# Side work of a causal attention block, moved to other units and in front of single maxima

## The chip, the core and the metric

The program runs on one core of a Trainium2 chip. A core has five engines, each with its own instruction queue: TensorE (PE in the profile, its weight loads apart as PEld), VectorE (DVE), ScalarE (ACT), GpSimd (POOL) and SyncE (SP), which here only issues transfers. An engine takes its instructions in the order of its queue, and waits on semaphores that other engines or transfers raise. The metric is the device time of one execution in microseconds (us); smaller is better.

## The reference

For x of 4 batches x 1024 rows x 128 columns, three residual blocks are computed in float32. The mixture-of-experts block stands before and after the attention.

```
x = x + 0.5 * ffn(layernorm(x))       # router top 2 of 8, 1280 places per expert, 128 -> 512 -> 128, exact gelu
x = x + attn(layernorm(x))            # 16 heads of 8, causal softmax, output projection
x = x + 0.5 * ffn(layernorm(x))       # same weights

# attn
q, k, v = split(x @ wq.T + bq), split(x @ wk.T + bk), split(x @ wv.T + bv)
scores  = einsum('bhsd,bhtd->bhst', q, k) / 8 ** 0.5, causal mask
ctx     = einsum(softmax(scores), v);  out = ctx @ wo.T + bo

# the router of ffn, for all 4096 rows n
logits = xt @ gate_w;  top_logits, top_idx = top_k(logits, 2);  weights = softmax of the two
rank of a row in its expert = number of rows before it that chose it (all first choices, then all second)
a choice counts if rank < 1280; out[n] = sum of its weights * expert output
```

## The kernel before, in words

The first ffn comes first, then the attention over the 4 batches, then the second ffn. The change touches the attention alone. It has 16 steps: batches 0 to 3, and in each the groups g = 0 to 3 of four heads. Batches 1 and 2 are the same code ("mid"), batch 0 is "first" and batch 3 "final".

A step has 12 units u. Units 0 to 3 are the first half of the queries with key blocks 0 to 3 (queries of width 512, 384, 256, 128), units 4 to 11 the second half with key blocks 0 to 7 (512 for units 4 to 8, then 384, 256, 128). In each unit PE makes two pairs of score blocks (L1489), ACT takes their exponentials (L1823), for the units on the diagonal (0 to 3 and 8 to 11) POOL puts the causal zeros in (L2252), and two units later PE multiplies them with the values (L1537, called "values" below). Beside this, the row maxima of the *next* step are computed: PE makes score blocks (L1505, diagonal mask L1514), and DVE reduces them (L1903, "a maximum" below). Units 0 to 11 hold 2, 2, 1, 1, 2, 2, 2, 2, 2, 2, 2 and 0 of the 20 maxima. POOL splits the maxima of a half into three bf16 parts (`split_max`, L2226 to L2230: half 1 of this step's successor at u = 11, half 0 at u = 7), PE turns them (L1548, at the ends of units 0 and 8), and SP moves them through memory into the query tiles.

Scores and maxima share a ring of three two-bank slots in PSUM, in the order score, maximum, score, maximum, so PE can write a block only when ACT or DVE has read the block three places earlier. One more bank (`c_bank`) serves all small tasks in a fixed order. At the end of unit 11 and of unit 2 DVE normalises the context (`context`, L1913 and L1915), which frees that bank for L1548.

The side work of the neighbouring batches is placed by conditions on (g, u) in each engine's `step`, as a rule *behind* the unit's exponentials or maxima:

- g = 0: POOL adds the expert outputs to x1 of the next batch; DVE takes its row statistics (`sums`, `moments`), POOL the root (`rstd1`), ACT normalises it (`norm`, L1797, 8 row tiles at u = 10 and 11). For the batch before, PE and DVE add the output projection (`add_out`), and DVE takes router statistics (`router_sums`, u = 8 to 11, then `router_moments`).
- g = 1: POOL takes the router's root, ACT normalises the router's rows (`norm_out`, L1808, u = 1 and 2); x, q and k tasks of the next batch at u = 3 to 10.
- g = 2: the router: logits on PE at u = 5, on DVE the first choice behind u = 6, the second behind u = 7, ranks behind u = 9, places behind u = 10, weights and row numbers behind u = 11.
- g = 3: 16 scatters of the router's rows on POOL (`router_scatter`, L404), 3 behind each of u = 0 to 3 and 1 behind each of u = 4 to 7; v tasks at u = 3 and 4.

A dependent chain of DVE operations runs through `Steps`: each call raises a semaphore and waits for it. It is written so, and the scatters are placed so:

```
def __call__(self, ins):
    ins.then_inc(self.s, 1)
    self.k += 1
    self.eng.wait_ge(self.s, self.base + self.k)
...
turns = range(3 * u, 3 * u + 3) if u < 4 else range(u + 8, min(u + 9, TOPK * T))
```

## Time and profile before

| | |
|---|---|
| three runs | 1027.87, 1031.98, 1039.04 us; median 1031.98 us |
| the profiled execution | 1036.6 us from its first to its last instruction (no other time is given for it) |
| attention, first exponential of batch 0 to that of the last step | 290.2 to 789.7 us |
| busy, whole span | PE 831.8 us (80%), DVE 601.5 (58%), ACT 523.4 (50%), POOL 489.6 (47%) |
| DVE L1903, the maxima | 320 instructions, 348.5 us |
| ACT L1823, the exponentials | 384 instructions, 300.4 us |
| POOL L404, the scatters | 48 instructions, 47.4 us |

The span is read by step: a step begins where ACT starts the exponentials of its unit 0. "[0.97 <-DVE ctx L1915]" behind a row means that the engine sat idle for 0.97 us before it, until that instruction was done. PEclk is the granted clock of TensorE, 1.00 for 2.4 GHz and 0.50 for 1.2 GHz.

### The profile page before, as it was taken

How to read it: one execution, taken by the hardware profiler on the slowest of the kernel's cores; microseconds unless marked ns; L12 is line 12 of the kernel's file. 1: busy time of each engine (PE TensorE's matmuls, PEld its weight loads, DVE VectorE, ACT ScalarE, POOL GpSimd, SP SyncE). 2: the span in 40 equal slices, each digit the busy share in tenths (PEclk: the TensorE clock that was granted, in tenths of full speed). 3: DMA queues.
4: the chain of work that ended last, by engine and by line, in shares of the span. 5: the costliest groups of instructions: out<-in, count | busy, mean ns of one | idle time of the engine just before them, and what ended most of it. 6: DMA issues, size and time to landing. Idle time of an engine off the chain costs nothing. (4 is left out here: it accounts for less than half of the span.)

```text
span 1036.6 us, 18080 instructions
## 1 busy us (share of the span) xinstructions
PE 831.8 (80%) x6599; PEld 446.5 (43%) x6599; DVE 601.5 (58%) x1237; ACT 523.4 (50%) x841; POOL 489.6 (47%) x686
## 2 busy tenths in 40 slices
PE   8569999944668988888978899878887618999990
PEld 7437878742212223332333323323232316787770
DVE  7931211124767788888787977878775423334235
ACT  6323343442237776777556786566766303433330
POOL 5047455325652662646467522562224651545453
PEclk9769999986657999999799999999899758999995
DMA  7115575621451262341524224323202124423236
GB/s 204 73 26 153 148 217 145 192 63 51 130 162 66 53 189 48 89 144 43 174 76 105 99 53 152 85 65 106 53 18 79 53 63 149 130 79 97 78 136 228
DMA packets 96185, 110.81 MB, mean 107 GB/s; under 512 B 12279, under 2 KB 68763, under 8 KB 96104
## 3 DMA queue, kind: packets, MB, share of 16 engines
q1 hardware_dynamic: 84752, 88.86, 29.1%
q0 software_dynamic: 9216, 17.98, 6.8%
q10 hardware_dynamic: 2136, 2.91, 0.8%
q8 instruction: 49, 0.80, 0.3%
q14 instruction: 32, 0.26, 0.1%
HBM read 57.86 MB, written 52.89 MB: 107 GB/s over the span
## 5 line engine op out<-in xcount | busy, mean ns | idle before, releaser
L1903 DVE TENSOR_REDUCE m_blk<-banks 128x8 f32<-128x1024 f32 (+1 forms) x320 | 348.5, 1114 | 79.7 <-PE banks L1505 67.1
L1823 ACT ACTIVATE pt<-banks 128x1024 f32<-128x1024 f32 (+3 forms) x384 | 300.4, 811 | 145.1 <-PE banks L1489 142.7
L1537 PE MATMUL banks<-pt,vs 128*32 128x512 f32 (+3 forms) x1536 | 176.6, 534 | 7.2 <-POOL pt L2252 3.8
L1489 PE MATMUL banks<-qb,kp 64*128 64x512 bf16 (+3 forms) x768 | 132.6, 351 | 53.7 <-DVE m_blk L1903 45.2
L2252 POOL TENSOR_SCALAR_AFFINE_SELECT pt<-pt 128x512 f32<-128x512 f32 x128 | 81.6, 637 | 192.1 <-ACT pt L1823 191.7
L1505 PE MATMUL banks<-kp,qa 64*128 64x128 bf16 (+4 forms) x1152 | 126.4, 294 | 19.6 <-ACT pt L1823 11.6
L849 POOL DMA_INDIRECT xe<-xn_rows,slot_tok x80 | 79.9, 999 | 94.4 <-PE banks L1190 37.2
L675 POOL DMA_INDIRECT y_tab<-ys,ids x70 | 68.0, 972 | 81.5 <-DVE ys L635 64.5
L1106 ACT ACTIVATE he<-banks,b_up 128x512 f32<-128x512 f32 (+1 forms) x96 | 57.9, 616 | 89.9 <-PE banks L1190 89.5
L1505 PEld LDWEIGHTS banks<-kp,qa 48*128 48x128 bf16 (+1 forms) x1152 | 46.2, 99 | 130.3 <-ACT pt L1823 92.7
L585 ACT ACTIVATE hT<-banks,bfc 128x512 f32<-128x512 f32 (+1 forms) x96 | 56.3, 615 | 84.9 <-DVE bfc L607 48.8
L1489 PEld LDWEIGHTS banks<-qb,kp 64*128 64x128 bf16 x768 | 36.1, 95 | 134.5 <-DVE m_blk L1903 89.5
L1190 PE MATMUL banks<-xeT,w_up 128*128 128x512 f32 (+1 forms) x192 | 76.3, 548 | 2.3 <-DVE xeT L1018 2.3
L1200 PEld LDWEIGHTS banks<-w_dn,he 128*128 128x128 f32 x640 | 73.9, 192 | 3.8 <-issue 3.8
L1200 PE MATMUL banks<-w_dn,he 128*128 128x128 f32 x640 | 75.2, 275 | 0.0
L632 DVE TENSOR_TENSOR ys<-banks,early_b 128x512 f32<-128x512 f32 (+1 forms) x24 | 14.5, 603 | 88.7 <-PE banks L543 88.7
L1027 DVE TENSOR_TENSOR ye<-banks,b_dn 128x512 f32<-128x512 f32 (+1 forms) x24 | 14.5, 603 | 83.2 <-PE banks L1200 83.2
L1537 PEld LDWEIGHTS banks<-pt,vs 128*32 128x32 f32 x1536 | 31.3, 111 | 54.1 <-issue 31.9
L404 POOL DMA_INDIRECT bucket<-rows,row_ix x48 | 47.4, 988 | 13.8 <-issue 13.8
L1190 PEld LDWEIGHTS banks<-xeT,w_up 128*128 128x128 f32 x192 | 37.2, 202 | 29.7 <-issue 24.2
L2265 POOL DMA_INDIRECT gy<-y_slots,y_row x32 | 32.6, 1018 | 36.0 <-POOLq L711 26.7
L1018 DVE COPY xeT<-banks 128x512 f32<-128x512 f32 (+1 forms) x24 | 14.3, 597 | 46.7 <-PE banks L1181 46.7
(344 smaller groups left out, 1128.8 us busy)
## 6 DMA issues: line engine op xcount, KB each, us to landing
bucket<-zero SPq DMA_DIRECT2D x16, 660.0 KB
qb<-q_stack SPq DMA_DIRECT2D x32, 192.0 KB, 3.5
qa<-q_stack SPq DMA_DIRECT2D x30, 192.0 KB, 3.3
kp<-k_stack SPq DMA_DIRECT2D x30, 192.0 KB, 4.2
q_stack<-qp SPq DMA_DIRECT2D x18, 256.0 KB
k_stack<-kq SPq DMA_DIRECT2D x18, 256.0 KB
y_slots<-ye SPq DMA_DIRECT2D x16, 256.0 KB, 2.5
mid<-x SPq DMA_DIRECT2D x8, 512.0 KB, 3.6
```

The source lines that it names most:

```text
L585: nc.scalar.activation(hT[par][:, b, 0:n * P], h_bank[b][:, 0:n * P], ACT.Gelu, bias=bfc[q][:, b:b + 1]).then_inc(h_done, 1)
L675: nc.gpsimd.indirect_dma_start(table[:, :], bass.IndirectOffsetOnAxis(ap=ids[q][:, t:t + 1], axis=0), ys[q][:, t, :], None, bounds_check=r ...
L849: nc.gpsimd.indirect_dma_start(xe[q][:, t, :], None, xn_rows[:, :], bass.IndirectOffsetOnAxis(ap=slot_tok[:, e * CT + t:e * CT + t + 1], a ...
L1106: nc.scalar.activation(he[par][:, b, 0:n * P], h_bank[b][:, 0:n * P], ACT.Gelu, bias=b_up[q][:, b:b + 1]).then_inc(up_done, 1)
L1190: nc.tensor.matmul(h_bank[b][:, 0:n * P], w_up[q][:, b * P:(b + 1) * P], xeT[q][:, t0 * P:(t0 + n) * P], start=True, stop=True).then_inc(u ...
L1200: i = nc.tensor.matmul(y_bank[par][:, t * P:(t + 1) * P], he[par][:, b, t * P:(t + 1) * P], w_dn[q][:, b, :], start=b == 0, stop=b == FB - 1)
L1489: i = nc.tensor.matmul(ring[SLOT["score", 2 * u + pair]][:, s, 0:w], kp[g][rows_s, pair, kb * P:(kb + 1) * P], qb[par][rows_s, pair, q0:q0 ...
L1505: i = nc.tensor.matmul(ring[slot][:, s, at:at + blocks * P], qa[par][rows_s, pair, qt * P:(qt + 1) * P], kp[g][rows_s, pair, kb * P:(kb + ...
L1537: i = nc.tensor.matmul(o_bank[VW * h:VW * h + VW, q:q + w], vs[par][:, kb, h, :], pt[u % PTS][:, h, 0:w], start=u in (0, SECOND), stop=u i ...
L1823: nc.scalar.activation(pt[u % PTS][:, 2 * pair:2 * pair + 2, 0:w], ring[SLOT["score", 2 * u + pair]][:, :, 0:w], ACT.Exp, scale=SCALE).the ...
L1903: nc.vector.tensor_reduce(dst, ring[slot][:, :, 0:blocks * P].rearrange("p s (j k) -> p s j k", k=P), AX.X, ALU.max).then_inc(m_done, 1)
L2252: nc.gpsimd.affine_select(out=v, in_=v, compare_op=ALU.is_ge, fill=0.0, base=0, pattern=[[0, HS], [1, P]], channel_multiplier=-1).then_inc ...
```

## The change

`router_top2`, `router_second`, `router_rank`, `router_places` and `router_weights` become two generators, `router_choose` and `router_rank`. `Steps.later` puts the `yield` between an instruction and the wait for it, so that what the caller places there stands ahead of the wait. Four tables say which row tiles are handled in which (g, u). The number of instructions stays the same.

```diff
+            def later(self, ins):
+                ins.then_inc(self.s, 1)
+                self.k += 1
+                yield
+                self.eng.wait_ge(self.s, self.base + self.k)
...
+            NORM_AT = {(0, 10): (0, 3), (0, 11): (3, 5), (1, 2): (5, T)}
+            OUT_AT = {(1, 10): (0, 3), (1, 11): (3, 5), (2, 2): (5, T)}
+            SUMS_AT = {(6, 0): (0, 2), (6, 1): (2, HB), (7, 0): (HB, 6), (7, 1): (6, T)}
+            ROUTER_SUMS_AT = {(0, 9): (0, 2), (0, 10): (2, 4), (0, 11): (4, 6), (1, 3): (6, T)}
...
-                        if g == 0 and not bt.final and u >= 10:
-                            norm(b + 1, (u - 10) * T // 2, (u - 9) * T // 2)
-                        if g == 1 and not bt.first and 1 <= u <= 2:
-                            norm_out(b - 1, (u - 1) * T // 2, u * T // 2)
+                        if (g, u) in NORM_AT and not bt.final:
+                            norm(b + 1, *NORM_AT[g, u])
+                        if (g, u) in OUT_AT and not bt.first:
+                            norm_out(b - 1, *OUT_AT[g, u])
...
+                        if g == 2 and not bt.first and u == 6:
+                            out_task(at, "r_lg", b - 1)
+                        if g == 2 and not bt.first and u == 10:
+                            out_task(at, "r_rk", b - 1)
                         for m in range(M_FROM[u], M_FROM[u + 1]) if more else ():
+                            if not bt.first and ((g == 2 and 6 <= u <= 10) or (g == 3 and u == 2)):
+                                for _ in range(2):
+                                    next(held["run"], None)
+                            if g == 0 and not bt.final and (u, m - M_FROM[u]) in SUMS_AT:
+                                sums(b + 1, *SUMS_AT[u, m - M_FROM[u]])
+                            if g == 0 and not bt.final and u == 8:
+                                (moments, moments_end)[m - M_FROM[u]](b + 1)
                             reduce(n + 1, m, SLOT["max", m])
...
-                        if g == 0 and not bt.first and u == NU - 1:
+                        if g == 1 and not bt.first and u == 4:
                             router_moments(dve, (b - 1) * ROUTER_STEPS)
-                        if g == 1 and not bt.first and u == 0:
+                        if g == 1 and not bt.first and u == 8:
                             router_numbers(dve, 0, b - 1).then_inc(r_num, 1)
...
+                        if g == 2 and not bt.first and u in (9, 11):
+                            for _ in range(4 if u == 9 else 2):
+                                next(held["run"], None)
+                        if g == 3 and not bt.first and u == 2:
+                            for _ in held["run"]:
+                                pass
...
-                        if g == 1 and not bt.first and u == 0:
+                        if g == 1 and not bt.first and u == 5:
                             router_rstd(pool, b - 1)
                             router_shift(pool, b - 1)
-                        if g == 3 and not bt.first:
-                            if u == 0:
+                        if g == 3 and not bt.first and u > 2:
+                            if u == 3:
                                 wait_apart(pool, r_idx, b)
...
-                                turns = range(3 * u, 3 * u + 3) if u < 4 else range(u + 8, min(u + 9, TOPK * T))
+                                turns = range(3 * u - 9, min(3 * u - 6, TOPK * T))
```

On POOL, g = 3 of batches 1 and 2, from the mask of unit 0 of the step (before):

```order
L2252 AFFINE_SELECT pt<-pt 128x4x128 x2
L404 DMA bucket<-rows,row_ix 40960x132 x3
L2252 AFFINE_SELECT pt<-pt 128x4x128
L404 DMA bucket<-rows,row_ix 40960x132 x3
L2252 AFFINE_SELECT pt<-pt 128x4x128
L404 DMA bucket<-rows,row_ix 40960x132 x3
L2252 AFFINE_SELECT pt<-pt 128x4x128
L404 DMA bucket<-rows,row_ix 40960x132 x6
L2226 TENSOR_SCALAR m_neg<-m_of 128x16
...
L404 DMA bucket<-rows,row_ix 40960x132
L2245 COPY vs<-v_all 128x32x9
```

and with the change (L400 is the scatter, L2260 the mask, L2234 the first step of `split_max`, L2253 the copy of the values for the next step):

```order
L2260 AFFINE_SELECT pt<-pt 128x4x128 x5
L400 DMA bucket<-rows,row_ix 40960x132 x12
L2234 TENSOR_SCALAR m_neg<-m_of 128x16
...
L400 DMA bucket<-rows,row_ix 40960x132 x3
L2253 COPY vs<-v_all 128x32x9
L2260 AFFINE_SELECT pt<-pt 128x4x128
L400 DMA bucket<-rows,row_ix 40960x132
L2260 AFFINE_SELECT pt<-pt 128x4x128 x2
```

The first mask of the five is that of unit 11 of the step before. No scatter stands between the masks of units 0 to 3 any more; 12 stand ahead of `split_max` and 15 ahead of the mask of unit 8.

On DVE, the end of g = 0 and the start of g = 1 in batch 1 (before):

```order
L1908 TENSOR_REDUCE m_of<-m_blk 128x16
L277 BN_STATS stat<-x 128x6 x4
L285 BN_AGGR mv<-stat 128x2 x8
L288 TENSOR_SCALAR neg_mean<-mv 128x8
L289 TENSOR_SCALAR var_e<-mv 128x8
L1913 RECIPROCAL recip<-banks 128x16
L1915 TENSOR_TENSOR ctx<-banks,recip 128x4x32
L1903 TENSOR_REDUCE m_blk<-banks 128x2x3 x2
```

and with the change:

```order
L1910 TENSOR_REDUCE m_of<-m_blk 128x16
L284 BN_STATS stat<-x 128x6 x4
L1915 RECIPROCAL recip<-banks 128x16
L1917 TENSOR_TENSOR ctx<-banks,recip 128x4x32
...
L284 BN_STATS stat<-x 128x6 x2
L1905 TENSOR_REDUCE m_blk<-banks 128x2x4 x2
L292 BN_AGGR mv<-stat 128x2 x8
L295 TENSOR_SCALAR neg_mean<-mv 128x8
L296 TENSOR_SCALAR var_e<-mv 128x8
L1905 TENSOR_REDUCE m_blk<-banks 128x2x4 x2
```

The aggregation and the two operations behind it went from ahead of the context to unit 4 of g = 1, two of the statistics to unit 3.

On DVE, g = 2 of batch 1 from unit 6, with the change (before, the seven operations from L333 stood together, then two maxima, then the next seven):

```order
L333 TENSOR_SCALAR tok_id<-tok_id 128x8
L334 COPY lg<-banks 128x64
L340 TENSOR_REDUCE top<-lg 128x8
L1905 TENSOR_REDUCE m_blk<-banks 128x2x4
L341 TENSOR_TENSOR eq<-lg,top 128x64
L342 TENSOR_TENSOR cand<-eq,place 128x64
L1905 TENSOR_REDUCE m_blk<-banks 128x2x4
L343 TENSOR_REDUCE chosen<-cand 128x8
L344 TENSOR_TENSOR hot<-place,chosen 128x8x8
L1905 TENSOR_REDUCE m_blk<-banks 128x2x4
```

Two operations of the router now stand in front of each single maximum.

## Rows read from the trace of the kernel before

**Rows 1.** The page's first line: the profiled execution.

```profile
span 1036.6 us, 18080 instructions
```

**Rows 2.** Windows of whole steps (stretch, length, busy by engine, PEclk, DMA share, GB/s).

```profile
365.00:393.90 28.90, 24.14 (x262) 7.84 (x258) 23.28 (x27) 20.18 (x29) 15.62 (x27) 1.00 0.59 173
393.90:424.30 30.40, 25.79 (x278) 9.68 (x274) 24.40 (x29) 19.90 (x28) 7.60 (x19) 1.00 0.24 59
424.30:455.60 31.30, 27.99 (x294) 10.57 (x290) 28.15 (x56) 23.92 (x39) 20.87 (x32) 1.00 0.44 128
490.30:525.90 35.60, 32.85 (x302) 11.68 (x298) 27.21 (x47) 21.01 (x32) 15.74 (x28) 0.81 0.48 139
525.90:559.20 33.30, 25.39 (x278) 9.63 (x274) 25.31 (x35) 20.36 (x29) 23.40 (x35) 1.00 0.32 86
626.20:660.00 33.80, 28.93 (x302) 11.02 (x298) 26.95 (x47) 21.08 (x31) 7.54 (x19) 0.95 0.45 130
```

**Rows 3.** Timeline of ACT: start us, us, instruction [idle before]; starts of units 0 and 3.

```profile
626.17 1.94 ACT L1823 ACTIVATE pt<-banks 128x1024 f32<-128x1024 f32 x2 [1.09 <-PE banks L1489]
632.79 0.38 ACT L1823 ACTIVATE pt<-banks 128x256 f32<-128x256 f32 x1 [1.21 <-PE banks L1489]
...
455.56 1.91 ACT L1823 ACTIVATE pt<-banks 128x1024 f32<-128x1024 f32 x2
464.57 0.77 ACT L1823 ACTIVATE pt<-banks 128x256 f32<-128x256 f32 x2
...
590.43 1.92 ACT L1823 ACTIVATE pt<-banks 128x1024 f32<-128x1024 f32 x2
595.57 1.65 ACT L1808 ACTIVATE rows<-x,shift,rstd 128x128 f32<-128x128 f32 x4
600.06 0.38 ACT L1823 ACTIVATE pt<-banks 128x256 f32<-128x256 f32 x1 [0.34 <-PE banks L1489]
...
723.27 1.94 ACT L1823 ACTIVATE pt<-banks 128x1024 f32<-128x1024 f32 x2 [1.09 <-PE banks L1489]
733.59 0.38 ACT L1823 ACTIVATE pt<-banks 128x256 f32<-128x256 f32 x1 [0.34 <-PE banks L1489]
```

**Rows 4.** Timeline of DVE and PE at the start of g = 1, batch 3.

```profile
722.88 0.86 DVE L277 BATCH_NORM_STATS2 stat<-x 128x6 f32<-128x128 f32 x4
725.03 0.25 DVE L1913 RECIPROCAL recip<-banks 128x16 f32<-128x16 f32 x1
...
725.65 0.24 PE L1548 MATMUL banks<-identb,m_parts 128*48 128x128 bf16 x1 [0.97 <-DVE ctx L1915]
```

**Rows 5.** Timeline of DVE, g = 1 of batch 1, behind unit 5.

```profile
472.67 0.75 DVE L1989 SCALAR_TENSOR_TENSOR rest<-banks,bq_c,qp 128x512 f32<-128x512 f32 x1 [0.55 <-ACT qp L1772]
```

**Rows 6.** Timeline of PE in g = 2, batch 2.

```profile
648.76 0.39 PE L1489 MATMUL banks<-qb,kp 64*128 64x512 bf16 x2 [1.04 <-DVE m_blk L1903]
```

**Rows 7.** Timelines of POOL and PE in g = 3 of batch 1 (step from 525.9).

```profile
528.74 1.09 POOL L404 DMA_INDIRECT bucket<-rows,row_ix  x1 [0.20 <-issue]
550.55 0.22 POOL L2230 TENSOR_TENSOR m_parts<-m_neg,m_parts 128x16 bf16<-128x16 f32 x1
...
552.75 0.65 POOL L2252 TENSOR_SCALAR_AFFINE_SELECT pt<-pt 128x512 f32<-128x512 f32 x1
...
541.83 0.43 PE L1537 MATMUL banks<-pt,vs 128*32 128x128 f32 x8 [1.56 <-POOL pt L2252]
551.55 0.24 PE L1548 MATMUL banks<-identb,m_parts 128*48 128x128 bf16 x1
555.56 1.07 PE L1537 MATMUL banks<-pt,vs 128*32 128x512 f32 x8
```

**Rows 8.** The same places on PE in g = 3 of batch 0 (step from 393.9).

```profile
416.69 0.24 PE L1548 MATMUL banks<-identb,m_parts 128*48 128x128 bf16 x1
420.69 1.06 PE L1537 MATMUL banks<-pt,vs 128*32 128x512 f32 x8
```

**Rows 9.** Forms of instruction, 424 to 830 us (busy us, mean ns | idle before).

```profile
L404 POOL DMA_INDIRECT bucket<-rows,row_ix x48 | 47.4, 988 | 13.8 <-issue 13.8
```

More of the change, by code:

```diff
@@ L387, in router_places @@
+            nc.vector.tensor_tensor(tk, tk, rb[:, T * W:T * W + W], ALU.add).then_inc(evac, 1)
+            yield
+            yield from step.later(nc.vector.tensor_tensor(ranks[:], ranks[:], hot[:], ALU.mult))
+            yield from step.later(nc.vector.tensor_reduce(rank[:], ranks[:], AX.X, ALU.add))
             nc.vector.tensor_scalar(over[:], rank[:], float(CAP), SKIP, ALU.is_ge, ALU.mult)
-            step(nc.vector.tensor_tensor(place_in[:], rank[:], sign[:], ALU.mult))
-            step(nc.vector.scalar_tensor_tensor(place_in[:], chosen[:], -4.0 * CAP, place_in[:], ALU.mult, ALU.add))
@@ L390, in router_places @@
-            step(nc.vector.tensor_tensor(place_in[:], place_in[:], over[:], ALU.add))
-        def router_weights(dve, call, buf, step):
+            yield from step.later(nc.vector.tensor_tensor(place_in[:], rank[:], sign[:], ALU.mult))
+            yield from step.later(nc.vector.scalar_tensor_tensor(place_in[:], chosen[:], -4.0 * CAP, place_in[:], ALU.mult,
+                                                                 ALU.add))
+            yield from step.later(nc.vector.tensor_tensor(place_in[:], place_in[:], over[:], ALU.add))
@@ L393, in router_weights @@
             dve.wait_ge(r_exp, call + 1)
-            step(nc.vector.tensor_scalar(es[:], eg[:], 1.0, None, ALU.add))
-            step(nc.vector.reciprocal(gap[:], es[:]))
+            yield from step.later(nc.vector.tensor_scalar(es[:], eg[:], 1.0, None, ALU.add))
+            yield from step.later(nc.vector.reciprocal(gap[:], es[:]))
             nc.vector.tensor_copy(rows[buf][:, :, C_P0], gap[:])
@@ L2314, in step @@
                             mask(n, u)
+                        if g == 0 and not bt.final and u == 9:
+                            rstd1(b + 1)
                         if is_last(b, g) and u == 10:
```

94 lines of the change are left out of this document (36 added, 58 removed).

## The prediction, made before the changed kernel ran

> **What bounds the kernel now.** The profiled execution spans 1036.6 us [rows 1], above the median of the runs (1031.98), so I work out a difference on this trace and take it off the median. I read the windows by step first, then the timelines of ACT, DVE, PE and POOL where a step is longer than a plain one.
>
> A plain step, with hardly any side work, is g = 2 of batch 0: 28.9 us, of which PE is busy 24.1, DVE 23.3 and ACT 20.2 [rows 2]. No engine is full there. What bounds it is the ring of three slots: PE writes a block, ACT or DVE reads it, PE may write again. So side work costs nothing while it fits into an engine's idle time inside a unit, and costs its excess when it stands as a block in front of something that the ring waits for. The reader should see in rows 2 how far the other steps are from 28.9, or from 30.4 for g = 3 with its v tasks (batch 0, no router): 31.3 for g = 0 of batch 1, 35.6 and 33.8 for the router steps g = 2 of batches 1 and 2, 33.3 for g = 3 of batch 1. The first units of g = 1 stand out in ACT's timeline: from the start of unit 0 to that of unit 3 a step without normalisations takes 632.79 - 626.17 = 6.6 us; batches 1, 2 and 3 take 9.0, 9.6 and 10.3 [rows 3]. That is 9.1 us in all over plain.
>
> **A. Start of g = 1 (gain).** Two blocks make those 9.1 us. On DVE four statistics (0.86 us) and the aggregation chain behind them (725.03 - 722.88 - 0.86 = 1.3 us) stand ahead of the context; PE waited 0.97 us for the context in order to turn the maxima [rows 4]. On ACT two blocks of four `norm_out`, 1.65 us each or 0.41 an instruction, stand between exponentials [rows 3]. The change leaves the four statistics there and takes the 1.3 us and both ACT blocks away. What comes instead is three `norm` (3 x 0.41 = 1.2 us) behind unit 2, where ACT in the plain step is idle 1.21 us before unit 3 [rows 3]: hidden, and if it is not, PE's transposes at unit 3 are late by the excess. The 0.86 us of statistics against the 0.97 us that PE waits, less the 1.3 removed, makes PE's wait vanish, but the first maximum is still late; I take 0.45 us a batch as left. Gain 9.1 - 3 x 0.45 = 7.7 us. Bounds: none is saved beyond the 9.1; at worst the old cost stays where ACT work remains, about half, 4.5. Batch 0 loses half of its eight `norm` from the end of g = 0 as well; between nothing and the 3 x 0.41 moved away I take 0.7. A together: 8.4.
>
> **B. What g = 1 gets back (cost).** Two statistics (0.43) at unit 3 and the chain (1.3) at unit 4. In batches 1 and 2 DVE is idle 0.55 us behind unit 5, waiting for ACT's q part [rows 5], and the ring is held by ACT there, so I take 0.3 each. In batch 3 no q, k tasks run, and the step is as plain as a step is; there 1.7 us meet idle time of (28.9 - 23.3) / 12 = 0.5 us a unit [rows 2], so 1.0. `norm_out` behind units 10 and 11 (3 and 2 instructions, 1.2 and 0.8 us): plain idle time of ACT is (28.9 - 20.2) / 12 = 0.7 a unit, and unit 10 holds another cast in batches 1 and 2. Bounds 0 to 1.2 each; 0.4, as most of it is covered: 0.8. The last three stand behind unit 2 of g = 2, in the same 1.21 us as in A: 0. POOL's root and product at unit 5 stand ahead of nothing that is due before. B: 2.4 us of cost.
>
> **C. g = 0 (gain).** Batches 1 and 2: the step is 2.4 us over plain [rows 2], for PE's transposes, `add_out`, statistics and moments. The change only cuts the blocks of four statistics into twos in front of single maxima and the moments in two. Between 0 and 2.4, nearer to a third as the sum of DVE work is the same: 0.7 each, 1.4.
>
> **D. The router, g = 2 (gain).** The same DVE operations, in pairs of about 0.5 us instead of two blocks of about 1.6. In batch 2 PE waited 1.04 us for a maximum behind such a block [rows 6]. But a pair in front of a maximum in each of seven to eight places also makes DVE's period longer than its 0.5 us of idle time a unit covers, so most of the block's price comes back as many small ones. Between -1.0 and +1.0 us a step, I take a gain of 0.4 for each of three steps: 1.2. The logits on PE and what they do to the clock (0.81 and 0.95 in the two windows of rows 2) stay. On the waits inside the chain the Trainium skill speaks ("VectorE: DVE Perf Modes", "The DRAIN you can't avoid"): a semaphore between two DVE operations adds no time of its own. By it D would be 0.9, as a third of my gain is the hidden wait; the sum would move by 0.3.
>
> **E. g = 3 of batches 1 and 2 (cost).** This is the part that I trust most. Before, POOL starts the scatters 2.8 us into the step, and the masks of units 2 and 3 stand behind them: PE waited 1.56 us for one [rows 7]. The step takes 33.3 instead of 30.4 [rows 2]. Now POOL does the four masks first, and then 12 scatters, `split_max`, 3 scatters, the copy and the mask of unit 8. When is it done? Scatters take (47.4 + 13.8) / 48 = 1.28 us each in a row [rows 9]. In a plain step the exponentials of unit 3 start 6.6 us in, the second ends about 0.9 later (two of 0.38 and a gap, an estimate), the mask takes 0.65: the first scatter is at 8.5. From the first scatter to the end of `split_max` it was 550.77 - 528.74 = 22.0 us with 15 scatters and three masks; less 3 x 1.28 and 3 x 0.7 it is 16.3 (gaps between them leave 16.6). So the parts of the maxima are ready at 25.1. PE wants them at 416.69 - 393.9 = 22.8 in a step that nothing holds up [rows 8]; before, it came for them at 25.6 [rows 7]. **PE stalls 2.3 us at unit 8.** Then three scatters, copy and mask: before, 2.6 us with one scatter, so 5.2, and the mask of unit 8 ends at 30.3. PE's values for unit 8 want it at 420.69 - 393.9 = 26.8, plus the 2.3, that is 29.1; **1.2 us more**. The step comes to 30.4 + 3.5 + 0.2 for the weights' operations in front of unit 2 = 34.1, against 33.3: 0.8 worse, although the old stall is gone. The earlier context at its start (nine operations on DVE ahead of it become two) is already in the 30.4. To this I add 0.8 for the clock, which fell in some places where PE stood (rivals). E: 2 x 1.6 = 3.2 us of cost; bounds -2.9 (no stall at all) and +6 a step. Batch 3's last step has no maxima; its eight scatters keep their place: 0.
>
> **The sum.** -8.4 + 2.4 - 1.4 - 1.2 + 3.2 = -5.4 us. On the profiled execution 1031.2; on the median **1026.6 us**. The rest of the program is untouched, and the attention's end moves the second ffn's start as it is.
>
> **The rivals.**
>
> R1, *POOL's queue becomes the bound and the clock falls with it* (slower). Each stall of PE in g = 3 leaves it idle; if TensorE is granted 1.2 GHz afterwards, its values go at half speed through units 9 to 11 and into the next step. Price from rows: the router step at clock 0.81 is 1.8 us longer than that at 0.95 [rows 2]; two stalls, each with such a fall, make E's step 0.8 + 2 x 1.8 = 4.4, and a later start of the scatters (row numbers late, or a mask late) adds a us for each us. At 6 a step and with A only half as large the sum is -4.5 + 2.4 - 1.4 - 1.2 + 12 = +7.3: 1039. It decides from 1.6 + 2.7 = 4.3 us a step on. For it: the two router steps lost clock although PE is busier there than in a plain step [rows 2]. Against: in rows 7 PE waited 1.56 us and the window reads 1.00. The Trainium skill ("TensorE: Matmul & The Clock Gate", "HAM oscillation") says that a kernel whose TensorE keeps pausing for another unit falls back to 1.2 GHz again and again. By that rule R1's price comes due each time; the trace agrees only for some pauses. Chance 0.14.
>
> R2, *E costs nothing and the clock gains* (faster still). If DVE or ACT hold PE back so that it comes to unit 8 at 25 anyway, the stall is hidden, and E is -1.0 a step for the missing waits; with A's starts also go the falls of the clock, and D is worth 1.0 a step. -8.4 + 2.4 - 1.4 - 3.0 - 2.0 = -12.4: 1019.6. Against it: a plain g = 3 reaches unit 8 at 22.8. Chance 0.22.
>
> R3, *the work only changes places*. DVE's total is the same, and every unit of g = 1 and g = 2 has little idle time left; then A's gain is given back in units 3 to 11: -1 to -2 in all, 1030.5. For it: DVE is busy 27 to 28 us in each such step. Against: the waits at the start of g = 1 are for blocks that are gone. Chance 0.16.
>
> The forecast itself has 0.48.
>
> **The numbers.** The range reaches from R2's neighbourhood up into R1's: 1017 to 1037; the forecast's own runs from 1022 to 1031. Within 1% of 1031.98 is 1021.7 to 1042.3, about what a measurement tells from no change. Below it lie R2 and the lower tail of the forecast: 0.27. Above lies the tail of R1: 0.07. Between: 0.66.
>
> **What the profile would show.** A: units 0 to 2 of g = 1 take 7 us instead of 9 to 10 in batches 1 to 3, and no wait of L1548 for the context is left there. B: waits for maxima at units 4 and 5 of g = 1, in batch 3 above all. D: waits for maxima below 1 us through units 6 to 8 of g = 2, the step 33 to 35 as before. E: in g = 3 of batches 1 and 2 no wait of values for a mask at units 4 and 5, but one of 2 to 2.5 us at L1548 behind unit 8 for POOL's parts and one of about a us of values for the mask of unit 8; the step 34 to 36 us. I am wrong if g = 3 is below 32, if the starts of g = 1 stay above 8.5, or if the span outside the attention moves.

## The result

The changed kernel took 1020.0 us in the median of four runs (1017.33 to 1024.78), the kernel before beside it 1031.09 (1027.87 to 1039.04). The ratio is 0.9866, 95% interval 0.9823 to 0.9909: faster by 1.3%. The forecast was 1026.6 us. Two later comparisons of the same two kernels gave 0.9882 (0.9839 to 0.9925) and 0.9877 (0.9831 to 0.9923). A ratio with its interval is worked out from the single executions and need not be the quotient of two medians. Medians are over executions in the chip's faster state; of one version below (half of D) two of twelve executions, at 1035.77 and 1039.03 us, were in the slower one and are left out.

The profiled execution spans 1020.6 us, 16.0 less than [rows 1]. Not all of that is the change. Attention begins (first exponential of batch 0) at 284.1 us instead of 290.2, and the code up to there is the same; from there to the last step's start it is 489.0 us instead of 499.5; the rest is 247.5 against 246.9. Leave out g = 0 of batch 0 as well, whose length varies with no edit near it (below), and it is 447.2 against 458.1: **10.9 us** in the steps that the prediction speaks of.

### The profile page after: what moved, and what is told of

Read it like the earlier page. It is cut to its first block and busy times, and to the rows that moved or that the text cites. A ratio compares the mean times of both kernels' runs of the same rounds, so it can differ in the third digit from the quotient of the medians.

```text
span 1020.6 us, 18073 instructions
## 1 busy us (share of the span) xinstructions
PE 822.9 (81%) x6599; PEld 442.1 (43%) x6599; DVE 598.4 (59%) x1237; ACT 522.6 (51%) x841; POOL 489.6 (48%) x686
## 5 line engine op out<-in xcount | busy, mean ns | idle before, releaser
L1533 PE MATMUL banks<-pt,vs 128*32 128x512 f32 (+3 forms) x1536 | 174.5, 528 | 2.5 <-ACT o_sb L1765 2.4
L2260 POOL TENSOR_SCALAR_AFFINE_SELECT pt<-pt 128x512 f32<-128x512 f32 x128 | 81.4, 637 | 178.7 <-ACT pt L1825 178.6
L845 POOL DMA_INDIRECT xe<-xn_rows,slot_tok x80 | 79.9, 999 | 88.1 <-PE banks L1186 34.3
L1186 PE MATMUL banks<-xeT,w_up 128*128 128x512 f32 (+1 forms) x192 | 73.7, 533 | 2.3 <-DVE xeT L1014 2.3
L400 POOL DMA_INDIRECT bucket<-rows,row_ix x48 | 48.0, 1000 | 15.0 <-issue 14.1
L1533 PEld LDWEIGHTS banks<-pt,vs 128*32 128x32 f32 x1536 | 31.0, 110 | 48.4 <-issue 32.3
L2273 POOL DMA_INDIRECT gy<-y_slots,y_row x32 | 32.4, 1014 | 35.9 <-POOLq L707 26.7
```

Of the source, the lines that this page charges most:

```text
L845: nc.gpsimd.indirect_dma_start(xe[q][:, t, :], None, xn_rows[:, :], bass.IndirectOffsetOnAxis(ap=slot_tok[:, e * CT + t:e * CT + t + 1], a ...
L1186: nc.tensor.matmul(h_bank[b][:, 0:n * P], w_up[q][:, b * P:(b + 1) * P], xeT[q][:, t0 * P:(t0 + n) * P], start=True, stop=True).then_inc(u ...
L1533: i = nc.tensor.matmul(o_bank[VW * h:VW * h + VW, q:q + w], vs[par][:, kb, h, :], pt[u % PTS][:, h, 0:w], start=u in (0, SECOND), stop=u i ...
L2260: nc.gpsimd.affine_select(out=v, in_=v, compare_op=ALU.is_ge, fill=0.0, base=0, pattern=[[0, HS], [1, P]], channel_multiplier=-1).then_inc ...
```

## The profile after

First the page's first line and PE's row in it, then windows of whole steps (stretch, length, busy time by engine PE, PEld, DVE, ACT, POOL, granted clock, DMA share, GB/s). They are g = 0 to 3 of batch 1, g = 2 of batch 2, g = 1 and g = 2 of batch 3, and answer to [rows 1, 2].

```profile
span 1020.6 us, 18073 instructions
...
PE 822.9 (81%) x6599; PEld 442.1 (43%) x6599; DVE 598.4 (59%) x1237; ACT 522.6 (51%) x841; POOL 489.6 (48%) x686
```

```profile
417.70:448.60 30.90, 27.10 (x286) 10.44 (x282) 26.96 (x50) 22.83 (x36) 20.31 (x29) 1.00 0.42 125
448.60:482.60 34.00, 30.57 (x278) 10.06 (x274) 28.24 (x48) 27.76 (x46) 22.58 (x36) 0.95 0.30 68
482.60:516.70 34.10, 31.29 (x302) 11.65 (x298) 26.69 (x47) 22.27 (x34) 15.59 (x27) 0.85 0.49 145
516.70:551.20 34.50, 28.50 (x278) 10.18 (x274) 25.36 (x36) 19.85 (x28) 23.52 (x36) 0.90 0.35 98
614.90:647.00 32.10, 28.69 (x302) 11.02 (x298) 26.51 (x48) 22.26 (x35) 7.32 (x18) 0.95 0.47 138
711.10:742.40 31.30, 25.13 (x262) 7.90 (x258) 24.82 (x44) 22.26 (x33) 9.45 (x22) 0.95 0.23 57
742.40:773.10 30.70, 27.27 (x300) 10.88 (x296) 26.41 (x47) 22.17 (x34) 7.53 (x20) 1.00 0.05 11
```

Read length and clock together. g = 2 of batch 2 takes 32.1 us where it took 33.8 at the same clock of 0.95 [rows 2]: that is the change. g = 3 of batch 1 takes 34.5 at 0.90 where it took 33.3 at 1.00: PE is busy 3.1 us longer there with the same 278 instructions, because part of them ran at 1.2 GHz.

**Start of g = 1, batch 3**, timelines of DVE, PE and ACT, against [rows 3, 4]:

```profile
710.73 0.86 DVE L284 BATCH_NORM_STATS2 stat<-x 128x6 f32<-128x128 f32 x4
711.51 0.24 DVE L1915 RECIPROCAL recip<-banks 128x16 f32<-128x16 f32 x1
...
712.47 0.24 PE L1544 MATMUL banks<-identb,m_parts 128*48 128x128 bf16 x1
713.00 0.34 PE L1485 MATMUL banks<-qb,kp 64*128 64x384 bf16 x2 [0.29 <-DVE m_blk L1905]
...
711.12 1.94 ACT L1825 ACTIVATE pt<-banks 128x1024 f32<-128x1024 f32 x2 [1.09 <-PE banks L1485]
718.01 0.38 ACT L1825 ACTIVATE pt<-banks 128x256 f32<-128x256 f32 x1 [1.21 <-PE banks L1485]
```

From statistics to reciprocal it is 0.78 us instead of 2.15. PE no longer waits for the context, and unit 3 begins 718.01 - 711.12 = 6.9 us in (10.3 before). The clock is in these 3.4 us as well. The two windows, units 0 to 2 of g = 1 in batch 3, first before and then changed:

```profile
723.27:733.59 10.32, 8.26 (x77) 3.19 (x73) 7.33 (x22) 8.33 (x17) 5.60 (x12) 0.67 0.42 107
```

```profile
711.12:718.01 6.89, 5.75 (x77) 2.36 (x73) 5.88 (x11) 5.26 (x8) 3.76 (x10) 1.00 0.29 75
```

PE is busy 2.5 us longer in the first with the same 77 instructions. In batches 1 and 2 the granted clock of these units was 0.81 and 0.66 before, 0.79 and 1.00 with the change.

**g = 2, units 6 and 7 of batch 2**, timeline of DVE in the changed kernel:

```profile
627.99 1.23 DVE L1905 TENSOR_REDUCE m_blk<-banks 128x8 f32<-128x1024 f32 x1 [0.22 <-PE banks L1501]
629.87 0.17 DVE L333 TENSOR_SCALAR tok_id<-tok_id 128x8 f32<-128x8 f32 x1 [0.65 <-PE banks L328]
...
630.20 0.22 DVE L340 TENSOR_REDUCE top<-lg 128x8 f32<-128x64 f32 x1
630.50 1.23 DVE L1905 TENSOR_REDUCE m_blk<-banks 128x8 f32<-128x1024 f32 x1
631.64 0.21 DVE L341 TENSOR_TENSOR eq<-lg,top 128x64 f32<-128x64 f32 x1
631.89 0.22 DVE L342 TENSOR_TENSOR cand<-eq,place 128x64 f32<-128x64 f32 x1
633.33 1.23 DVE L1905 TENSOR_REDUCE m_blk<-banks 128x8 f32<-128x1024 f32 x1 [1.22 <-PE banks L1501]
```

The first operations of the router lie between maxima where DVE was waiting for PE anyway, and 1.22 us of waiting are still left behind the second pair. This stretch ran at half clock.

**g = 3, batch 1** (step from 516.7), timelines of POOL and PE, against [rows 7]:

```profile
524.35 0.63 POOL L2260 TENSOR_SCALAR_AFFINE_SELECT pt<-pt 128x512 f32<-128x512 f32 x1 [1.50 <-ACT pt L1825]
525.19 1.09 POOL L400 DMA_INDIRECT bucket<-rows,row_ix  x1 [0.20 <-issue]
...
539.37 0.97 POOL L400 DMA_INDIRECT bucket<-rows,row_ix  x1 [0.30 <-issue]
...
541.56 0.22 POOL L2238 TENSOR_TENSOR m_parts<-m_neg,m_parts 128x16 bf16<-128x16 f32 x1
...
546.31 0.65 POOL L2260 TENSOR_SCALAR_AFFINE_SELECT pt<-pt 128x512 f32<-128x512 f32 x1
```

```profile
541.92 0.27 PE L1544 MATMUL banks<-identb,m_parts 128*48 128x128 bf16 x1 [2.28 <-POOL m_parts L2238]
...
543.20 1.94 PE L1533 MATMUL banks<-pt,vs 128*32 128x512 f32 x8
...
547.01 1.64 PE L1533 MATMUL banks<-pt,vs 128*32 128x512 f32 x8
547.01 0.20 PEld L1533 LDWEIGHTS banks<-pt,vs 128*32 128x32 f32 x8 [0.29 <-POOL pt L2260]
```

The first scatter starts 8.5 us in, the parts are ready at 25.1, the mask of unit 8 ends at 30.3, PE waits 2.28 us: the forecast's own numbers. The values at 543.20 take 1.94 us where an undisturbed group takes 1.06 [rows 8]. The second wait of the forecast, about 1.2 us of the values for the mask of unit 8, is nearly gone: no matmul waits for it, and the weight load of these values only 0.29 us.

## The experiments

The time of each version stands beside runs of the kernel before on the same chip. "The changed kernel again", A, B and C alone, "without D" and "spread scatters" ran on one chip; half of D, the two with A undone in part or whole, and the first "late scatters" on a second; the third run of the changed kernel and the last three versions on a third. Edits are cut, and told in words where they are long. For the steps I use the starts of ACT's unit 0 in each profile's timeline. All in us; "from g = 1 of batch 0" is up to the last step's start.

| profile | first exp. | g=0, batch 0 | g=1, batches 1/2/3 | g=2, batches 1/2/3 | g=3, batches 1/2 | from g=1 of batch 0 |
|---|---|---|---|---|---|---|
| before | 290.2 | 41.4 | 34.7 / 35.7 / 32.6 | 35.6 / 33.9 / 33.8 | 33.3 / 33.3 | 458.1 |
| changed | 284.1 | 41.8 | 34.0 / 32.8 / 31.3 | 34.1 / 32.1 / 30.7 | 34.5 / 34.2 | 447.2 |
| changed, again | 289.0 | 42.8 | 34.0 / 32.8 / 31.3 | 34.2 / 32.1 / 30.7 | 34.4 / 34.2 | 447.2 |
| changed, third | 284.3 | 42.2 | 32.8 / 32.8 / 31.3 | 31.9 / 32.2 / 30.7 | 34.4 / 34.1 | 443.7 |
| A, B, C alone | 288.7 | 39.1 | 34.0 / 32.8 / 31.1 | 35.5 / 33.7 / 32.1 | 33.3 / 33.3 | 449.4 |
| changed without D | 289.4 | 38.9 | 32.8 / 32.8 / 30.0 | 33.4 / 32.1 / 32.1 | 35.6 / 37.4 | 449.7 |
| half of D, early scatters | 290.3 | 39.7 | 34.3 / 32.8 / 32.5 | 32.2 / 32.0 / 30.7 | 33.3 / 37.3 | 448.7 |
| statistics back | 290.5 | 39.7 | 35.2 / 36.3 / 34.0 | 30.7 / 32.3 / 35.3 | 34.2 / 34.0 | 455.5 |
| A, B undone | 284.6 | 43.4 | 35.4 / 35.2 / 31.9 | 32.3 / 32.2 / 32.3 | 33.9 / 35.4 | 456.3 |
| spread scatters | 290.7 | 40.6 | 34.1 / 32.8 / 30.0 | 35.3 / 34.3 / 30.7 | 30.5 / 30.5 | 448.1 |
| late scatters | 289.0 | 43.2 | 32.8 / 32.8 / 31.1 | 32.1 / 32.1 / 35.2 | 30.5 / 30.5 | 440.6 |
| late scatters, again | 289.2 | 42.9 | 32.8 / 34.1 / 35.1 | 31.9 / 35.3 / 30.7 | 30.5 / 30.5 | 444.3 |
| late scatters without D | 287.5 | 39.0 | 32.8 / 32.8 / 30.0 | 33.4 / 33.6 / 32.1 | 33.5 / 31.2 | 442.8 |
| before, late scatters | 290.3 | 41.3 | 34.4 / 35.6 / 34.1 | 32.4 / 34.0 / 35.2 | 32.6 / 32.5 | 457.1 |

### The changed kernel again

> The changed kernel once more, so that the runs beside it are compared on one chip. By the two traces the attention is 10.5 us shorter than before and the other 6 us of the two spans' difference (1036.6 and 1020.6) lie in the first ffn, whose code is the same. Theory 1, the 6 us are chance of an execution: they don't come back, and the difference of the medians is 8 to 12 us. Theory 2, the start of the program does depend on the change: the attention starts near 284 us again and not near 290, and the difference is 14 to 16 us.

1024.91 us against 1034.62, ratio 0.9882 (0.9839 to 0.9925): 9.7 us. The start of attention is at 289.0 now and was at 284.1. Theory 1 holds: the 6 us ahead of attention were chance, and every step behind g = 0 of batch 0 reproduced to 0.1 us. (In the third run the attention began at 284.3 us again.)

### A, B and C alone

```
-(g == 2 and 6 <= u <= 10) ... next(held["run"], None)   # pairs in front of maxima
+(u in (6, 7, 9, 10, 11)): all of a unit's router operations behind its maxima
-turns = range(3 * u - 9, min(3 * u - 6, TOPK * T)), from u = 3
+turns = range(3 * u, 3 * u + 3) if u < 4 else range(u + 8, ...), from u = 0
```

> The kernel before with A, B and C alone: normalisations, statistics, moments and the root of the router where the change puts them, router operations in blocks and scatters from unit 0 as before. By the steps of the two traces g = 0 and g = 1 gave 0.9 + 0.4 + 0.7 + 0.4 + 2.9 + 1.3 = 6.6 us. Theory 1, the parts add up: 6 to 7 us faster than before. Theory 2, what A takes away is paid back in g = 2 (the last three normalisations stand in its unit 2): g = 2 gets longer by 1 us a step and the gain is 3 to 4 us. Theory 3, the forecast's sum of A, B and C: 7.4 us.

1024.89 us, ratio 0.989 (0.9846 to 0.9934). By steps 449.4 against 458.1: 8.7 us, of which 1.7 in g = 2 of batch 3 are a fall of the clock that did not happen there. So the rest is 7.0: theory 1, though theory 3's 7.4 is too near to be told from it. This median is that of the whole change beside it (1024.91): what D and E do together can't be seen in the total.

### The changed kernel without D

```
+if g == 2 and not bt.first and u in (6, 9):
+    out_task(at, {6: "r_lg", 9: "r_rk"}[u], b - 1)
+if g == 2 and not bt.first and u in (6, 7, 9, 10, 11):
+    for _ in range({6: 6, 7: 9, 9: 3, 10: 3, 11: 9}[u]):
+        next(held["run"], None)
```

> The changed kernel with only the router's operations of g = 2 back in blocks behind the maxima of units 6, 7, 9, 10 and 11 (D undone; the scatters stay behind unit 3). Theory D, pairs in front of single maxima are hidden whole: g = 2 of batches 1 to 3 goes back from 34.1, 32.1 and 30.7 to 35.6, 33.9 and 33.8 us, the kernel is 5 to 6.5 us slower than the changed one. Rival, the forecast's own size (0.4 a step): 1 to 1.5 us slower. Rival 2, the gain of g = 2 is that the clock fell at other places: some of the three steps come back longer and others not, and which ones follows the clock and not the order. g = 3 of batches 1 and 2: the weights' operations at unit 2 go, the scatters start no earlier: 34.2 to 34.5 as in the changed kernel.

1026.94 us, ratio 0.9918 (0.9886 to 0.9951): 2.0 us behind the changed kernel, with intervals that overlap; no theory's number for the total is confirmed. Nor did its three router steps come back longer one by one: 33.4, 32.1 and 32.1 us against 34.2, 32.1 and 30.7, since the clock fell less in them (0.90, 1.00 and 1.00 against 0.85, 0.95 and 1.00). That is what the second rival said. The windows settle the size at an equal clock. Windows of g = 2 in three kernels: this one, batch 3; A, B, C alone, batches 1 and 3; half of D, batches 1 and 3.

```profile
745.80:777.90 32.10, 27.56 (x300) 10.85 (x296) 26.81 (x47) 22.16 (x34) 7.68 (x21) 1.00 0.04 9
```

```profile
484.50:520.10 35.60, 32.84 (x302) 11.74 (x298) 27.10 (x47) 22.23 (x35) 15.81 (x28) 0.81 0.48 140
745.10:777.20 32.10, 27.56 (x300) 10.85 (x296) 26.80 (x47) 22.14 (x35) 7.72 (x20) 1.00 0.04 9
```

```profile
486.90:519.20 32.30, 28.69 (x302) 11.06 (x298) 26.55 (x47) 22.27 (x35) 15.60 (x27) 0.95 0.53 155
748.00:778.70 30.70, 27.27 (x300) 10.88 (x296) 26.40 (x47) 22.14 (x35) 7.52 (x19) 1.00 0.04 10
```

At clock 1.00 a router step takes 32.1 us with blocks and 30.7 with pairs; at 0.95 it is 33.8 [rows 2] against 32.1 to 32.3. **D is worth 1.4 to 1.7 us a step at an equal clock.** The clock adds a second effect of the same size that comes and goes: the kernels with blocks show 32.1 to 35.6 us for the same instructions, those with pairs 30.7 to 35.3. On the mean of all profiles in the table the three router steps take 97.4 us with pairs (nine profiles) and 100.6 with blocks (five), 3.2 us less, and the two groups overlap. Without D, g = 3 of batches 1 and 2 took 35.6 and 37.4 us, not the 34.2 to 34.5 that I expected: with the block of weights back in front of it, unit 0 takes 2.74 us instead of 1.97, and in both batches the clock fell once more, in the first units.

Where the 1.4 us come from, the same place in the kernel with A, B and C alone shows (timeline of DVE, g = 2 of batch 3, unit 6, at clock 1.00):

```profile
760.60 1.23 DVE L1905 TENSOR_REDUCE m_blk<-banks 128x8 f32<-128x1024 f32 x1 [1.20 <-PE banks L1501]
762.13 1.22 DVE L1905 TENSOR_REDUCE m_blk<-banks 128x8 f32<-128x1024 f32 x1 [0.31 <-PE banks L1501]
763.27 0.16 DVE L333 TENSOR_SCALAR tok_id<-tok_id 128x8 f32<-128x8 f32 x1
```

DVE stands idle for 1.20 and 0.31 us ahead of the two maxima of unit 6 and begins the block only behind them. The pairs fill these idle times: the maxima of unit 6 start where they did, and the first of unit 7 starts 18.6 us into the step instead of 19.7. Units 7 and 8 take 3.03 and 3.20 us instead of 4.12 and 3.44. Where the clock had fallen, as in batch 3 of the kernel before, the idle times were longer:

```profile
771.53 1.23 DVE L1903 TENSOR_REDUCE m_blk<-banks 128x8 f32<-128x1024 f32 x1 [1.35 <-PE banks L1505]
774.37 1.22 DVE L1903 TENSOR_REDUCE m_blk<-banks 128x8 f32<-128x1024 f32 x1 [1.61 <-PE banks L1505]
```

### Half of D with early scatters

```
-if g == 2 and not bt.first and u in (9, 11): range(4 if u == 9 else 2)
+if g == 2 and not bt.first and u in (9, 11): range(4 if u == 9 else 12)
-g = 3: two operations in front of each maximum of unit 2, scatters from unit 3
+g = 3: none; scatters 3 a unit from unit 0, as before
```

> The changed kernel with the second half of the router chain (ranks, places, weights) finished in unit 11 of g = 2 and the scatters from unit 0 of g = 3 on, as before; the first half still stands in pairs in front of single maxima in units 6 to 9. Theory, first half of D is worth its 1.3 us in unit 7 (2.84 against 4.15) whatever stands behind: unit 7 of g = 2 is 2.8 to 3.0 us; the block at unit 11 costs 0.8 to 1.0 at the start of g = 3 (unit 0 takes 2.75) and the masks of units 2 and 3 another 2: g = 3 of batches 1 and 2 takes 33.3 instead of 34.4 and 34.2, the kernel is 1 to 2 us faster than the changed one. Rival, the place of the scatters is all that matters in g = 3: with the scatters early it is 31 to 32. Rival 2, the block at unit 11 is longer than before, since more of the chain is in it: g = 3 at 34.5 or more, no gain.

1025.53 us against 1035.1, ratio 0.9917 (0.9878 to 0.9956). g = 2 is 32.2, 32.0 and 30.7, and its unit 7 took 2.8 to 3.0 us as expected: the first half of the chain carries all that D gives inside g = 2. Unit 0 of g = 3 takes 2.73 us, and the step 33.3 in batch 1, as the theory said; in batch 2 it was 37.3, with the clock at half speed in its first units and again later (0.77 over the step). The changed kernel did not run on this chip; by the ratios, 0.9917 against 0.9866 to 0.9882, the expected gain of 1 to 2 us did not come.

### Which block made the start of g = 1 slow

```
-ROUTER_SUMS_AT = {(0, 9): (0, 2), (0, 10): (2, 4), (0, 11): (4, 6), (1, 3): (6, T)}
+ROUTER_SUMS_AT = {(0, 8): (0, 2), (0, 9): (2, 4), (0, 10): (4, 6), (0, 11): (6, T)}
-g == 1 and u == 4: router_moments; u == 8: router_numbers; u == 5: root and shift (POOL)
+g == 0 and u == 11: router_moments; g == 1 and u == 0: router_numbers, root and shift
```

> The changed kernel with only DVE's and POOL's router statistics back at the end of g = 0 and the start of g = 1 (sums at units 8 to 11 of g = 0, aggregation at its unit 11, row numbers, root and shift at unit 0 of g = 1), while ACT's normalisations stay where the change puts them. Theory ACT (its two blocks of four made the start of g = 1 slow): units 0 to 2 of g = 1 take 7.2 to 7.5 us in batches 1 to 3. Theory DVE (the aggregation chain ahead of the context did): 8.0 to 8.5 us. The forecast of A held both to share the 9.1 us and did not split them. Units 3 to 5 of batch 3's g = 1 take 0.85 us less than in the changed kernel if the chain at unit 4 is what made them longer (2.40 and 3.08 against 2.17 and 2.46).

One run, 1032.46 us, and one profile. Units 0 to 2 of g = 1 took 9.3, 10.3 and 10.3 us: theory DVE, and more than its number. Batch 2, timelines of DVE and PE:

```profile
583.46 0.86 DVE L284 BATCH_NORM_STATS2 stat<-x 128x6 f32<-128x128 f32 x4
584.36 0.64 DVE L292 BATCH_NORM_AGGREGATE mv<-stat 128x2 f32<-128x6 f32 x8
585.03 0.60 DVE L295 TENSOR_SCALAR neg_mean<-mv 128x8 f32<-128x8 f32 x1
...
585.90 0.29 DVE L1917 TENSOR_TENSOR ctx<-banks,recip 128x128 f32<-128x128 f32 x1
```

```profile
586.25 0.24 PE L1544 MATMUL banks<-identb,m_parts 128*48 128x128 bf16 x1 [0.98 <-DVE ctx L1917]
587.11 0.34 PE L1485 MATMUL banks<-qb,kp 64*128 64x384 bf16 x2 [0.63 <-DVE m_blk L1905]
```

ACT had none of its blocks of four there, and yet the 0.98 us of waiting [rows 4] and the length are back, with a granted clock of 0.81, 0.67 and 0.70 in these units. The edit also brings back the row numbers and POOL's two operations; the wait that is seen is for DVE's context. Units 4 and 5 of batch 3 took 2.18 + 2.45 us against 2.40 + 3.08, the expected 0.85 less.

### A and B undone

```
+NORM_AT = {(0, 10): (0, HB), (0, 11): (HB, T)}
+OUT_AT = {(1, 1): (0, HB), (1, 2): (HB, T)}
```
(and the statistics as in the experiment before)

> The changed kernel with A and B undone altogether: statistics as in the experiment before, and the normalisations back in blocks of four (units 10 and 11 of g = 0, units 1 and 2 of g = 1). C, D and E stay. Theory, A and B are worth what the steps of the two traces say: units 0 to 2 of g = 1 take 9.0, 9.6 and 10.3 us again in batches 1 to 3, the step 34.7, 35.7 and 32.6. Rival, the start of g = 1 was slow because of the clock of the step before: the units come out at other values than these, within 7 to 9.

One run, 1031.2 us. Units 0 to 2 took 9.3, 9.3 and 9.7 us, the steps 35.4, 35.2 and 31.9: the old lengths within 0.7. With ACT's blocks on top the start is no longer than without them. **The chain on DVE is enough to make the start slow, and ACT's blocks add nothing to it.** Whether they would cost something with the chain gone was not tried, and these are two single profiles, in which the clock differs too (0.64, 0.63 and 0.82 here).

### Scatters spread

```
+TURNS = [0, 0, 0, 0, 3, 5, 7, 9, 10, 12, 14, 16, 16]
-turns = range(3 * u - 9, min(3 * u - 6, TOPK * T))
+turns = range(TURNS[u], TURNS[u + 1])
```

> The changed kernel with the scatters of g = 3 spread: 3 at unit 3, 2 at units 4 to 6 each (9 instead of 12 ahead of the negated maxima's split), 1 behind the split (3), 2, 2, 2 behind the masks of units 8, 9 and 10. Theory S, POOL's queue causes both stalls at unit 8 (2.28 us at the turn of the maxima, then the mask of unit 8): 9 scatters end at 525.2 + 9 x 1.28 = 536.7, the split at 538.2, before PE wants it (539.6), so g = 3 of batches 1 and 2 takes 30.5 to 31.5 us instead of 34.5 and 34.2, and the kernel is 6 to 7 us faster than the changed one. Rival, PE gets to unit 8 early only because nothing held it before: the ring or the clock takes the time instead, g = 3 stays at 33 to 34 and the gain is below 2 us. Rival 2, the masks of units 9 and 10 or the wait for the last scatters at unit 11 are late instead: a wait of PE for a mask moves to units 10 and 11, the gain is 3 us.

1024.89 us, ratio 0.9881 (0.9828 to 0.9933): no gain over the changed kernel. g = 3 is 30.5 us twice, as short as without a router, but g = 0 behind it takes 34.8 and 32.5 instead of 30.9 and 29.9. Timeline of POOL, then of PE, at the end of the step (one line was added, so a mask is L2261 here and the last part L2239):

```profile
554.91 0.98 POOL L400 DMA_INDIRECT bucket<-rows,row_ix  x1 [0.30 <-issue]
555.90 0.31 POOL L2235 TENSOR_SCALAR m_neg<-m_of 128x16 f32<-128x16 f32 x1
...
558.75 0.63 POOL L2261 TENSOR_SCALAR_AFFINE_SELECT pt<-pt 128x512 f32<-128x512 f32 x1 [0.82 <-DMA bucket<-rows,row_ix]
```

```profile
557.48 0.27 PE L1544 MATMUL banks<-identb,m_parts 128*48 128x128 bf16 x1 [2.19 <-POOL m_parts L2239]
```

The 2.28 us wait at unit 8 became one of 2.19 at the next step's unit 0. Sixteen scatters from unit 3 on don't fit into what is left of the step.

### Late scatters

```
+TURNS = [0, 0, 0, 0, 3, 5, 7, 9, 10, 11, 12, 12, 12]
+if g == 0 and b > 1 and u == 7:
+    for k in range(TURNS[NU], TOPK * T):
+        router_scatter(pool, 0, k)
+if g == 0 and b > 1 and u == NU - 1:
+    wait_apart(pool, scattered[0], 16 * TOPK * T * (b - 1))
```

> The spread kernel had g = 3 of batches 1 and 2 at 30.48 us, but the next step's units 0 to 2 at 10.6 and 9.1 instead of 6.6 us: POOL's queue was still full at unit 11, the second split came late and PE waited 2.19 us for it. Here 12 scatters stand in g = 3 (3 at unit 3, 2 each at units 4 to 6, 1 each at units 7 to 9) and the last 4 at unit 7 of the next step, g = 0, where POOL was idle for 6.9 us; the wait for their landing moves to unit 11 of that step. Theory, it was POOL's queue alone: g = 3 is 30.5, g = 0 of batches 2 and 3 is 30.9 and 29.9, so the attention is 3.9 + 3.6 = 7.5 us shorter than the changed kernel's, and the kernel at 0.980 to 0.982 of before. Rival, TensorE's clock takes it: with no stall the granted clock falls elsewhere (half-clock stretches in g = 0 or g = 1), each costs 1.3 to 1.7 us, gain 2 to 4 us. Rival 2, the scatters at unit 7 of g = 0 hold back the mask of unit 8 or the root at unit 9: g = 0 gets longer by 1 to 3 us.

1016.73 us against 1035.1, ratio 0.9814 (0.9767 to 0.9861). Windows of g = 3 in batch 1, g = 0 in batch 2, g = 3 in batch 2, g = 2 in batch 3; then PE at unit 8:

```profile
519.80:550.30 30.50, 25.90 (x278) 9.68 (x274) 25.17 (x36) 19.98 (x29) 19.67 (x32) 1.00 0.31 86
550.30:581.10 30.80, 27.01 (x286) 10.43 (x282) 26.86 (x49) 22.80 (x35) 24.20 (x33) 1.00 0.46 134
...
646.00:676.50 30.50, 25.89 (x278) 9.68 (x274) 25.16 (x36) 19.95 (x29) 19.68 (x32) 1.00 0.30 84
737.50:772.80 35.30, 32.76 (x300) 11.50 (x296) 26.65 (x48) 22.06 (x35) 7.59 (x20) 0.81 0.03 9
```

```profile
542.65 0.24 PE L1544 MATMUL banks<-identb,m_parts 128*48 128x128 bf16 x1
```

PE waits for nothing there, and g = 0 is as short as it was. POOL's queue made E's cost in these steps.

> The kernel with 12 scatters in g = 3 and 4 at unit 7 of the next g = 0, a second time. Theory, the 7 us over the changed kernel are its removed waits and not chance: 0.979 to 0.983 of before and 5 to 9 us under the changed kernel on the same chip. Rival, chance of the clock: under 3 us.

The second time, beside the changed kernel, it was 1021.94 us, ratio 0.9855 (0.9802 to 0.9908), and not faster than that one. g = 3 is 30.5 us again in both batches, 7.6 less in all. But the whole from g = 1 of batch 0 on is 440.6 and 444.3, against 447.2, 447.2 and 443.7: on the mean 3.6, about the difference between two profiles of one kernel. In the first run g = 2 of batch 3 took 35.3 at clock 0.81 where it took 30.7 at 1.00; in the second, g = 1 of batch 3 took 35.1 and g = 2 of batch 2 35.3. The rival holds in part: in these profiles about half of what the waits cost is found again as falls of the clock at other places. A gain in the total over the changed kernel is not shown.

> The changed kernel a third time, as the measure for the three beside it on one chip: 0.986 to 0.989 of before.

1020.26 us against 1038.0, ratio 0.9877 (0.9831 to 0.9923).

### Late scatters without D, and on the kernel before

The diffs are those of "late scatters" and of "without D" together, and of "late scatters" on the kernel before.

> The same late scatters with the router operations back in blocks (A, B, C and the repaired E, without D). By the steps: g = 2 costs 1.4 to 1.6 a step more at an equal clock, three times, and the block at unit 11 costs 0.8 at the start of g = 3, twice: 4.2 to 4.8 + 1.6 = about 6 us slower than the kernel beside it (0.986 to 0.988 of before). Rival, the forecast's size of D (0.4 a step): 1 to 2 us slower, 0.982 to 0.984.

1015.39 us, ratio 0.982 (0.9768 to 0.9871), beside 1021.94 (0.9802 to 0.9908) for its twin that has D: the intervals overlap, and it is not 6 us slower. g = 2 takes 33.4, 33.6 and 32.1, and g = 3 33.5 and 31.2, so the 1.4 and the 0.8 us a step are there. They are made up for elsewhere: its g = 0 of batch 0 took 39.0 us against 43, in code that is the same, and the clock fell in fewer of the later steps (granted clock over the span 0.915, against 0.898 and 0.892). From g = 1 of batch 0 on it is 442.8 us, between the twin's 440.6 and 444.3. I can't say whether that is chance.

> The kernel before with its scatters alone moved: from behind unit 3 of g = 3 and 4 of them into unit 7 of the next g = 0. Theory, the masks of units 2 and 3 waited only behind scatters: g = 3 of batches 1 and 2 takes 30.5 + 0.8 = 31.3 instead of 33.3 us, 4 us in all, 0.995 to 0.997 of before. Rival, the 33.3 of before is mostly the block of router weights at the end of g = 2: g = 3 stays above 32.3 and the gain is under 2 us.

1031.63 us, ratio 0.9954 (0.9923 to 0.9984). g = 3 is 32.6 and 32.5 instead of 33.3: 0.8 a step, not 2.0, and within the rival's bounds (above 32.3, and 1.0 us in all from g = 1 of batch 0 on). The masks' waits are gone, but unit 2 takes 4.05 us where a step without a fall takes 2.60, with a lower clock behind the block of weights; before, batch 2 alone had that. In the kernel above, batch 2 showed no such fall and the expected 31.2.

## Why the prediction was right, and where not

The direction was right and the size half of what came: -5.4 us forecast, -10.9 by the steps. The median of 1020.0 lies in the range, though outside the forecast's own part of it (1022 to 1031) and next to R2's 1019.6; that the range held is owed to the room it left for R2. One of its signs of being wrong came up: the span ahead of the attention moved by 6 us. The runs after showed that to be chance. The terms:

| term | forecast | measured, first trace |
|---|---|---|
| A and B | -8.4 + 2.4 = -6.0 | -0.9 - 0.7 - 2.9 - 1.3 = -5.8 |
| C | -1.4 | -0.4 - 0.4 = -0.8 |
| D | -1.2 | -1.5 - 1.8 - 3.1 = -6.4 |
| E | +3.2 | +1.2 + 0.9 = +2.1 |
| sum | -5.4 | -10.9 |

**A was near in size, half right in cause.** Units 0 to 2 took 7.0 us less in the three batches (7.7 forecast), and g = 1 of batch 0 0.9 less (0.7). It put the 9.1 us down to two blocks. DVE's chain alone brings them back, and ACT's blocks on top of it add nothing. Nor did the forecast ask what the clock did there: the three starts ran at 0.81, 0.66 and 0.67, two of them at 1.00 with the change. Batch 1 starts slowly still (8.1 us at 0.79, 6.9 in the third run at 1.00).

**B.** The statistics at units 3 and 4 cost 0.23 + 0.62 = 0.85 in batch 3 (1.0 forecast) plus a fall of the clock in unit 6 (4.17 us instead of 2.60), and nothing in batches 1 and 2; `norm_out` behind units 10 and 11 moved 0.2 us from one unit to the other: 0 instead of 0.8.

**C** was 0.4 a step instead of 0.7.

**D is the term that was mis-sized**: "most of the block's price comes back as many small ones", 0.4 a step. At an equal clock it is 1.4 to 1.7, about 4.6 in all (an estimate); the rest of the 6.4 is the clock, of g = 2 in batch 3 above all, where kernels with blocks took 33.8 with a fall and 32.1 without. I held the pairs against the mean idle time of a plain step, 0.5 us a unit. What counts is the idle time ahead of the maxima in those very units: 1.20 and 0.31 us at full clock. The trace of before has such rows, 1.35 and 1.61 us at half clock. Its sign, "the step 33 to 35 as before", failed in two steps of three.

**E's first wait came as worked out, the second hardly.** Scatters at 8.5, parts at 25.1, 2.28 us of PE's waiting and the mask at 30.3 are as forecast, and the step is 34.5 and 34.2 against 34.1 + 0.8. The forecast's own terms give these times only nearly: 6.6 + 0.9 + 0.65 is 8.2 and not 8.5, and 22.0 - 3.8 - 2.1 is 16.1 and not 16.3 or 16.6, which would make the wait 1.5 us. So close an agreement has luck in it. Of the 1.2 us of waiting for the mask of unit 8 only 0.29 are there. PE came to it later than forecast, for the clock fell towards the end of the first wait: against g = 3 of batch 0 (30.5 us) units 8, 9 and 10 of batch 1 take 2.54, 0.81 and 0.64 us more, and PE is at half speed in most of the last two. E also depends on D: without D the same scatters cost 2.3 and 4.1 us a step (33.3 to 35.6 and 37.4), since D takes the weights' block away from the start of g = 3. To count the two apart was too simple; together they are -2.2 by the steps (449.4 to 447.2), which the medians can't show.

**The rivals.** R1's mechanism is there: PE's wait of 2.28 us is followed by values at half speed (1.94 instead of 1.06 us). But a step became 1.2 and 0.9 us longer, not the 4.4 of R1, and A was not halved. R2's number came true though its first reason failed: E did cost. Its other two, that the falls of the clock at A's starts go and that D is worth 1.0 a step, were nearer to the runs than the forecast. R3 is refuted for A in batches 1 and 2, where units 3 to 11 are as long as before; in batch 3, 2.1 of the 3.4 us came back, 0.85 for the statistics and the rest where the clock fell.

**What stays open.** Why the falls of the clock move to other steps when a wait is taken away. The length of g = 0 of batch 0 goes with its granted clock: 0.75 to 0.76 in the three kernels with A and with blocks, which took 39 us, 0.70 at 39.7, 0.66 to 0.68 at 40.6 to 41.8, and 0.62 to 0.63 at 42.2 to 43.4. Why the clock differs there, though this stretch holds none of the router's work, is not known. What ACT's blocks cost without DVE's chain is open too. Whether D pays in the total is therefore not shown; that it pays in its steps is.
